# Local softmax: row sums from one VectorE reduction per tile in place of the exponentials' accumulators

## The chip, the cores and the metric

The kernel runs on one NeuronCore of a Trainium2 chip. TensorE (PE) multiplies matrices into PSUM, VectorE (DVE), ScalarE (ACT) and GpSimd (POOL) compute elementwise, and SyncE (SP) issues the transfers. Each engine works through its own instructions in order and waits for the others on semaphores. The metric is the device time of one execution in microseconds (us).

## The reference

The input is 8 sequences of 512 rows with 128 features. Four blocks follow each other, each with a residual and a layer norm in front of it: a small attention of which only the diagonal counts, two layers of a local-attention transformer (8 heads of 64), an attention with 16 heads of 8, and a mixture of 8 experts with a shared one. The change lies in the local attention:

```
bq = q.reshape(b, h, w, WINDOW, d) * QK_SCALE          # WINDOW = 64
bk, bv = (look_around(bk), look_around(bv))            # a window and the one before it: 128 keys
sim = einsum('bhwid,bhwjd->bhwij', bq, bk)
sim = where(mask, -max, sim)
attn = softmax(sim, axis=-1)                           # rows of 128
out = einsum('bhwij,bhwjd->bhwid', attn, bv)
```

The other softmaxes of the program (the diagonal one, the causal one with 16 heads, the router) are computed elsewhere and are not touched.

## The kernel before

The first two blocks are the "front" half (labels F), the last two the "back" half (labels B). Each engine's program is made of two lanes, one a front, one a back half, that work on different sequences at the same time. Each half is cut into named pieces, and a string of the letters F and B for each engine (ORDER) says from which lane the next piece comes. That order is fixed when the program is written; an engine that waits in a piece of one lane does nothing for the other. The strings have three parts: a first stretch, a turn that repeats five times (front of one sequence, back of the one before it), and a last stretch. In the first stretch two fronts run beside each other; in the last, two backs for a part of it.

The local attention of a sequence and layer has 4 tiles m of 128 rows. In one tile 8 heads lie side by side, so its scores are 128 x 1024, in two PSUM banks; four banks hold two tiles. There are 8 x 2 softmaxes, 64 tiles and 512 exponentials of 128 x 128. The pieces of a tile are these:

- sm (PE, lines 536 to 554): mask and scores into the banks of parity m. For m >= 2 it waits until the exponentials of tile m - 2 have left the banks.
- sm (DVE, lines 1108 to 1116): the negated row maxima of the 8 heads (L1111) and their product with the query's inverse norms, the bias of the exponentials (L1115).
- exm0, exm1 (ACT, L870): four exponentials each. Scale and bias are columns of tiles, and accum_out writes each one's row sums into `psum_`. In the trace each is an ACTIVATE and an ACTIVATION_READ_ACCUMULATOR. The eighth raises `l_exp`.
- rp (DVE, L1106): waits for `l_exp`, takes the reciprocals of the 8 sums, 128 x 8, and raises `l_rec`.
- sm, pt1 (POOL, L1400): waits for `l_rec` and multiplies the tile's probabilities by them (128 x 1024), and raises `l_pn`.
- pt (PE, L460): turns the tile's 8 blocks into two banks; pt0 also waits for the exponentials of tile 2, pt1 for those of tile 3, since they use their banks. ACT (L877) and DVE (L1123) copy the two banks out. pt2 and pt3 wait for the copies of the tile before.
- pv (PE) and its copy (ACT, L881), then wo (the output projection, residual added by DVE in L1137 and L1138), mean, var and the feed-forward.

Around them lie, in a turn: while layer 0's softmax runs (.0), the back lane starts a sequence: ln, xn (DVE, L1022; its rstd comes from POOL, L1346), tp and qkv (PE, with copies on ACT, L930 to L935), and parts, parts1 to parts3 (DVE, L1188 to L1197), which split q and k in three bf16 parts and release the transfer of SP (L1477) and behind it 24 more (L1485, L1488) that pack them. max0 to max21 for two rounds (PE scores, DVE row maxima, L1222) use the packed data. While layer 1's softmax runs (.1), the back lane is in its exponentials (ACT, L945, 40 of 128 x 512) and products, then oc (ACT, L948), turn0 to turn3 (PE L736, DVE L1231 and L1233), otp, wo. The rest of a turn is the experts' matmuls (moe, dn) beside the front's feed-forward and the next sequence's embedding and projections.

The program with the lines of the profile:

Of the kernel before, what the change touches and what calls it, by code (L numbers as in the profile page):

```python
# [52 lines left out]
FRONT_ENTERED = 6  # L53
# [3 lines left out]
        "FFFFBFFFBBBBFBFFBFFFFFBBFBFFBFFBFFBBFFFBFFBBBFFFFFFFBBBBBBFFBFFBBFFFFBBFFBFBBFFBFBFFBBFBFFFFBFFFFFBB"  # L57
        "BBBBFBFBBFBBFBFFBFFFFFBBFFBBBFBBBFBBFFFFBFFFFBBFFBFBFBBBFFFBBBBBFBFFFFFFBBBFBBBBFFFFFBFF",
        "FFBBFFFFFFFFFFFFFBBBBFBBBBBBBBBBBBFBBBFBBBFFBFBBFBBBBFBBBBFBFBBBBBFBBBFBBBFBBBBFBBBBBBBBBBBBBFBBBBBF"
        "FBBBFBBBBBBFFBBBFBBFBFBBFBBBBBBBBBBBBBFBBFBBBBBBBFBFBFFFFFFBFBBBFBBBBBBBBFBBFBBBBBFFFBFFFBFBFBBBBFBF"  # L60
        "FBFFFFBBBBBBFBFFBFBFBFBFBBBBBFFFFBFBFFFB",
        "FFBBFFFFBBBBBBBBBBBBBBBBBBBBFBBBBBBBBBBBBBBBBBBFBBBBFBBBBBBBBFBBBFBBBFBBBBBBFBBBFBBBBBFBBBBBBBBBBFBB"
        "BBBBBBBBBBBBBBBBFFBBBBFBBBBFBFFBFBBBBBFFBBBBBBBBBBBFFBBBBBFFBBBBBFBBFBBBBBFFFBBBBBFBBBBFBFFBBBFBFBBF"
        "FFFFFFFFFFBBBBFBBBBBBBBBBBBFBBBBBBBBBBBBBBFBBBBBBFBBBFFBBBFBBBFBBBBFBBBBFBBBBBBBBBFBBBBBBBBFBBBBBBBB"
        "BBBBBBBBBBBBBBBBBBBBBBBBBBBBBBFFFBBFFBBBBFBFBBFFFBBBBBBBBFBFFBBFFBFBFBBFBFFFFBFBBFFBBFFFFBBFFFBBFFBB"
        "FBFFBFFFBFFBFFBBFBBFFFBBFFFFFFFFBFFFFFFFFFFFFFFFFFFFFFFFFFFFFFFFFFFFFFFFFFFFFFFFFFFFFFFFFFFFFFFFFFFF"
# [3 lines left out]
        "FFFFFFBBFFFFFFBBBFFFBFFFBFBBBBFBBFBBFBBBFFFFFFFBFFFFFFFBFBFFBBBBBBBFBFFBBBFBFFBBFBFFFBBFFBFFFFFFFBFB"  # L70
        "FFBBBBFFFFBFBBBFFBBBBFFBBFFFFBFFFBBBBFBFFBBFFFBBBBBFBBBFBBBBFFFFBBBFBFFFFFBFFFFFFBBFBFFFF",
        "FBBFFFFFFFFFFFFFFFFFFFFFFFFFFFFFFBBBBBBBBBBFFBBBBBFBBBBBBFFBBBFBBBBBBFBBFFBBBBBBBFBBBBFFFBFFBFFFFFFF"
        "FBBBBBBFBBFFBFFFBBFBFBFFFFBBFBFFFFFFFFBFFFBFBBFFFF",
        "BBFFFFFFFFFFFFBBFBBBFBBBBBFFBBBBBBBBBBBFBBBBBBBBBBBFBBBBBBBBFBBBFBBFFBBBBBFFFFBBBFFBBFFFFBBFBFFBBFFB"
# [4 lines left out]
        "BFFBFFFFFFFFBFBBBFFBFFFBBFBFFBFFFFBFBBFBBBFBFBFFBBFFFBFFBBFFFFBFBBBBBFBBFBFBBBBFFFBFBFFFFFFFFFBFFBFF"  # L79
        "FFBFFBBBFFBFFBBFBFBBBFFBFBBFFBBBBFBFBBBFBFBFFBFBFFBBFBFBBBBFFFFFFFBFBFFBFFFFFFFFBFBBFBFFFBF",  # L80
        "BFFBBBFBFBFFBFFFFFFFFBBBBBBBBBBBFBBBBBBBBBBFBBFBBFBBBBFBBBBFBFBBBBFFBBBBBBBFFFBFFFFFFFFFFFFFFFFBBBBF"
        "FFBBFFBBBBBBBBBFBFBBBBFFFFBBBFFFBFBBFFBFFFFFFBFBBFFBFBFFFBFFFFBFFBFFBBBFFB",
        "BBBBBBFFFFFFFFBFFBBBBBBBBBBBBBBBBBBBBBBBBBBBBBBBBBBBBBBBBBBBBBFBFFFFBBBBFFFBBBFBBBBBBBFBBFFBBFFBBFBB"
        "BFFBBFBFFBFFBBBBBBFBFBBFFBBFFBBFBFBBBBFFFFFBFFFBBBBFBBBBBBBBBBBBBBBBBBBBBFBBBBBBBBBBBFBBBBBBBBBFFFBF"
        "FFFFFFFBBBBBBFFBBBBBBBFBFFFFFBFBBFBBFFFBFFBFBFBFFBBBFFFFBFFFBFFFFBFFBBFFBFFFFFBFBFFFFFBBBFBFFFFFFFFF"
        "FFFFFFFFFFFFFBFFFFFFFFFFFFFFFFF",
# [1499 lines left out]
```

## Time and profile before

| | before |
|---|---|
| median of 3 runs | 1870.97 us (1866.75 to 1878.17) |
| the profiled execution's own time | 1869.64 us |
| its span (first to last instruction) | 1867.5 us |
| busy: PE, DVE, ACT, POOL | 85%, 62%, 52%, 32% of the span |
| mean granted clock of TensorE | 0.946 |
| chain that ended last: PE, DVE, ACT, POOL | 49%, 19%, 17%, 10% |

The span is what the trace covers; the 2.1 us beside it are launch and end. The chain is followed back from the last instruction, at each step to what released it or to the instruction before it on its engine. Its shares say how long each engine was the one that the end waited for. The five repeated turns show the same pattern; the normalisation that begins one (L1022) starts at 527.96 us and the next at 749.92 us.

### The profile page before, as it was taken

Reading aid. Unit: us, or ns where it says so; the run is one execution under the profiler, and the core shown is the slowest. Engines: PE = TensorE matmul, PEld = TensorE weight load, DVE = VectorE, ACT = ScalarE, POOL = GpSimd, SP = SyncE. Lnnn points to the kernel's source line nnn. Section 1 sums busy time; section 2 is a strip of 40 time slices with the busy share of each in tenths; the row PEclk is TensorE's granted clock in tenths of the full one; section 3 lists DMA queues with packets and bytes.
Section 4 is the critical chain, followed back from the end, with each engine's and each line's share of the span. In section 5 each row is a group of like instructions: output and inputs, shape, how many; then the busy total and the mean of one; then the engine's idle time right before and its main releaser. Section 6 shows DMA issues by size and latency. Waiting matters only on the chain.

```text
span 1867.5 us, 30040 instructions
## 1 busy us (share of the span) xinstructions
...
## 2 busy tenths in 40 slices
...
DMA packets 37293, 80.13 MB, mean 43 GB/s; under 512 B 6782, under 2 KB 22654, under 8 KB 33776
## 3 DMA queue, kind: packets, MB, share of 16 engines
q1 hardware_dynamic: 37152, 78.22, 15.9%
...
## 4 chain that ended last, share of the span: by engine, by line
PE 49%; DVE 19%; ACT 17%; POOL 10%; issue 4%; DMA 0%; SPq 0%; POOLq 0%; DVEq 0%; ACTq 0%
PE ps L455 42%; ACT work L870 6%; PE ps L460 6%; DVE bsmall L1222 5%; POOL fsmall L1346 5%; ACT bigs L945 5%; POOL work L1369 3%; POOL work L1380 2%; DVE fxn L1022 1%; DVE work L1077 1%; DVE fsmall L1111 1%; DVE work L1076 1%; ACT pqs L870 1%; DVE bxn L1022 1%; POOL bsmall L1346 1%
## 5 line engine op out<-in xcount | busy, mean ns | idle before, releaser
L1346 POOL TENSOR_TENSOR fsmall<-fsmall,consts 128x8 f32<-128x8 f32 (+1 forms) x140 | 199.8, 1438 | 328.1 <-DVE fsmall L1016 316.2
L455 PE MATMUL ps<-maskb,identb 128*128 128x128 bf16 (+1 forms) x1118 | 226.4, 239 | 47.4 <-ACT work L870 36.8
L455 PE MATMUL ps<-bxt,mw 128*128 128x512 f32 x504 | 243.5, 600 | 5.9 <-DVE bigs L1318 5.9
L1369 POOL TENSOR_TENSOR work<-work 128x1024 f32<-128x1024 f32 x56 | 132.6, 2368 | 343.9 <-DVE work L1077 343.0
L870 ACT ACTIVATE work<-ps,fsmall 128x128 f32<-128x128 f32 x448 | 200.0, 504 | 32.3 <-DVE fsmall L1115 31.7
L460 PE MATMUL ps<-ident,work 128*128 128x128 f32 x924 | 141.3, 299 | 51.6 <-ACT work L870 31.5
L1222 DVE TENSOR_REDUCE bsmall<-ps 128x1 f32<-128x512 f32 (+3 forms) x308 | 174.8, 633 | 4.8 <-PE ps L455 4.3
L1400 POOL TENSOR_TENSOR work<-work,fsmall 128x1024 f32<-128x1024 f32 x56 | 108.1, 1932 | 214.3 <-DVE fsmall L1106 214.3
L455 PE MATMUL ps<-wqkv,h 128*128 128x512 f32 x336 | 159.4, 604 | 12.5 <-ACT vs L830 6.3
L945 ACT ACTIVATE bigs<-ps 128x512 f32<-128x512 f32 x280 | 145.6, 639 | 25.3 <-PE ps L455 25.0
L460 PEld LDWEIGHTS ps<-ident,work 128*128 128x128 f32 x924 | 114.3, 153 | 83.7 <-ACT work L870 36.3
L455 PEld LDWEIGHTS ps<-maskb,identb 128*128 128x128 bf16 x1152 | 112.0, 100 | 77.2 <-issue 75.8
L967 ACT ACTIVATE bigs<-ps 128x512 f32<-128x512 f32 x126 | 74.7, 597 | 120.4 <-PE ps L455 120.0
L455 PEld LDWEIGHTS ps<-bxt,mw 128*128 128x128 f32 x504 | 88.9, 192 | 91.4 <-issue 76.8
L455 PEld LDWEIGHTS ps<-mw,bigs 128*128 128x128 f32 x1008 | 121.1, 192 | 23.3 <-issue 21.7
L455 PE MATMUL ps<-work,w 128*114 128x512 f32 (+1 forms) x252 | 122.4, 609 | 5.9 <-ACT work L910 3.5
L455 PE MATMUL ps<-pks,pqs 96*128 96x128 bf16 (+3 forms) x448 | 112.1, 314 | 16.8 <-DVE bsmall L1222 10.4
L455 PE MATMUL ps<-mw,bigs 128*128 128x128 f32 x1008 | 123.2, 275 | 0.0
L870 ACT ACTIVATION_READ_ACCUMULATOR work<-ps,fsmall 128x1 f32 x448 | 112.2, 250 | 0.0
L1318 DVE TENSOR_TENSOR bigs<-ps,bigs 128x512 f32<-128x512 f32 x126 | 85.7, 685 | 39.4 <-PE ps L455 24.1
L1111 DVE TENSOR_REDUCE fsmall<-ps 128x8 f32<-128x1024 f32 x56 | 68.3, 1219 | 66.7 <-PE ps L455 66.6
L455 PE MATMUL ps<-pqs,pks 128*128 128x256 bf16 (+3 forms) x420 | 100.4, 299 | 9.6 <-ACT bigs L945 7.8
...
## 6 DMA issues: line engine op xcount, KB each, us to landing
...
```

The source lines that it names most:

```text
L455: return nc.tensor.matmul(o, a, b, start=start, stop=stop, skip_group_check=True)
L460: i = nc.tensor.transpose(bank[:, tt * P:(tt + 1) * P], src(tt), ident[:, :])
L870: i = nc.scalar.activation(R.pr[:, m, a, p, :], R.fb[2 * (m % 2) + a][:, p * P:(p + 1) * P], ACT.Exp, bias=R.pbias[:, m, k:k + 1], scale=R ...
L945: nc.scalar.activation(R.big[n], R.bb[k % 3][:, :], ACT.Exp).then_inc(R.c_e.sem, 1)
L967: nc.scalar.activation(R.silu[e % 2][c], R.bb[n % 3][:, :], ACT.Silu).then_inc(R.m_silu.sem, 1)
L1022: i = ts(xn[:, tt, :], src[:, tt, :], mv[:, tt, 0:1], rs[:, 1, tt:tt + 1], ALU.subtract, ALU.mult)
L1111: nc.vector.tensor_reduce(R.pmax[:, m, :], R.fpair[m % 2].rearrange("p a (c b) -> p (a c) b", b=P), AX.X, ALU.max, negate=True).then_inc(R ...
L1222: nc.vector.tensor_reduce(R.cmax[:, r, heads[0]:heads[-1] + 1, t], R.bb[k % 4][:, 0:cols * len(heads)].rearrange("p (a b) -> p a b", b=col ...
L1318: tt_(R.hid[e % 2][c], R.bb[n % 3][:, :], R.silu[e % 2][c], ALU.mult).then_inc(R.m_hid.sem, 1)
L1346: return nc.gpsimd.tensor_tensor(out, x, consts[:, k:k + 1].broadcast_to([x.shape[0], x.shape[1]]), op)
L1369: nc.gpsimd.tensor_tensor(R.qk[:, m, :], R.qk[:, m, :], R.part[m % 2], ALU.add).then_inc(R.l_add.sem, 1)
L1400: nc.gpsimd.tensor_tensor(p3, p3, R.prec[:, m, :].unsqueeze(2).broadcast_to([P, HEADS, P]), ALU.mult).then_inc(R.l_pn.sem, 1)
```

## The change

In the local softmax the exponentials no longer have accum_out. In rp, before the reciprocals, DVE sums the tile's 8 x 128 probabilities from SBUF with one tensor_reduce, 128x8 from 128x1024, raises a count of its own semaphore chain and waits for it. The chain's count per sequence grows by 4 per layer. Nothing else is computed otherwise.

```diff
-        self.fv, self.fp = sig("front_vector", FRONT_ENTERED + 4 * LAYERS, kind=Chain), sig("front_gpsimd", 2, kind=Chain)
+        self.fv, self.fp = sig("front_vector", FRONT_ENTERED + 8 * LAYERS, kind=Chain), sig("front_gpsimd", 2, kind=Chain)
...
                             i = nc.scalar.activation(R.pr[:, m, a, p, :], R.fb[2 * (m % 2) + a][:, p * P:(p + 1) * P], ACT.Exp,
-                                                     bias=R.pbias[:, m, k:k + 1], scale=R.rn[:, m, 2 * p + a:2 * p + a + 1],
-                                                     accum_out=R.psum_[:, m, k:k + 1])
+                                                     bias=R.pbias[:, m, k:k + 1], scale=R.rn[:, m, 2 * p + a:2 * p + a + 1])
                     i.then_inc(R.l_exp.sem, 1)
...
                 def reciprocals(m):
                     dve.wait_ge(R.l_exp.sem, R.l_exp.at(s, 4 * l + m + 1))
+                    nc.vector.tensor_reduce(R.psum_[:, m, :], R.pr[:, m, :, :, :].rearrange("p a c b -> p (a c) b"), AX.X,
+                                            ALU.add).then_inc(R.fv.sem, R.fv.one())
+                    dve.wait_ge(R.fv.sem, R.fv.now(s))
                     nc.vector.reciprocal(R.prec[:, m, :], R.psum_[:, m, :]).then_inc(R.l_rec.sem, 1)
```

The strings of all five engines are new as well, in all three stretches. Their pieces are the same, and each lane keeps its own order; only the interleaving differs. Read as pieces, the places of a turn that the text speaks of are these (the piece in brackets is the front's or the back's, F or B):

```
ACT before: (F)ex00.0 (B)tp (B)qkv (F)ex01.0 (F)ex10.0 (F)ex11.0 (F)ex20.0 (F)ex21.0 (F)ex30.0 (F)ex31.0 (F)pt0.0 (F)pt1.0
ACT after:  (F)ex00.0 (F)ex01.0 (B)tp (F)ex10.0 (B)qkv (F)ex11.0 (F)ex20.0 (F)ex21.0 (F)ex30.0 (F)ex31.0 (F)pt0.0 (F)pt1.0

DVE before: (B)ln (F)sm0.0 (F)sm1.0 (B)xn (B)parts (B)parts1 (F)rp0.0 (B)parts2 (F)sm2.0 (B)parts3 (F)rp1.0 (F)sm3.0 (B)va (F)rp2.0 (F)pt0.0 (F)rp3.0 (F)pt1.0
DVE after:  (B)ln (F)sm0.0 (B)xn (F)sm1.0 (F)rp0.0 (B)parts (B)parts1 (B)parts2 (B)parts3 (F)sm2.0 (F)rp1.0 (F)sm3.0 (F)rp2.0 (F)pt0.0 (B)va (F)rp3.0 (F)pt1.0

PE, DVE before: (F)wo1.0 (F)mean.0 (B)max0.0 (B)max1.0 (B)max2.0 (B)max3.0 (then PE: (F)var.0)
PE, DVE after:  (F)wo1.0 (B)max0.0 (B)max1.0 (F)mean.0 (B)max2.0 (B)max3.0 (PE's (F)var.0 two pieces later)

DVE before: (F)sm3.1 (F)rp2.1 (B)turn0 (B)turn1 (B)turn2 (B)turn3 (F)pt0.1 (F)rp3.1 (F)pt1.1 (B)wo (F: pt2.1 after it)
DVE after:  (F)sm3.1 (F)rp2.1 (B)turn0 (B)turn1 (F)pt0.1 (B)turn2 (B)turn3 (F)rp3.1 (F)pt1.1 (B)wo (F)pt2.1
PE before:  (B)turn2 (B)turn3 (F)pt0.1 (B)otp (F)pt1.1 (B)wo (F)pv0.1 (F)pt2.1
PE after:   (B)turn2 (F)pt0.1 (B)turn3 (F)pt1.1 (B)otp (F)pv0.1 (B)wo (F)pt2.1

PE before:  (B)dn2 (F)w2.1 (B)moe40g (F)out
PE after:   (F)w2.1 (B)dn2 (F)out (B)moe40g
SP before:  (B)dn1 after (B)dn0, then (F)ln; (F)v23.0 before (B)dn7
SP after:   (F)ln after (B)dn0, then (B)dn1; (F)v23.0 after (B)dn7
```

## Rows read from the trace of the kernel before

**Rows 1.** The page, part 4: the whole chain by engine and line, shares of the span.

```profile
PE 49%; DVE 19%; ACT 17%; POOL 10%; issue 4%; DMA 0%; SPq 0%; POOLq 0%; DVEq 0%; ACTq 0%
PE ps L455 42%; ACT work L870 6%; PE ps L460 6%; DVE bsmall L1222 5%; POOL fsmall L1346 5%; ACT bigs L945 5%; POOL work L1369 3%; POOL work L1380 2%; DVE fxn L1022 1%; DVE work L1077 1%; DVE fsmall L1111 1%; DVE work L1076 1%; ACT pqs L870 1%; DVE bxn L1022 1%; POOL bsmall L1346 1%
```

**Rows 2.** Busy time by window: window, its us, engines busy (instructions), clock, DMA.

```profile
547.00:553.00 6.00, 5.10 (x46) 4.65 (x47) 1.03 (x3) 2.50 (x7) 1.90 (x1) 0.50 0.73 124
527.96:749.92 221.96, 194.33 (x1446) 114.93 (x1454) 138.93 (x319) 122.59 (x285) 73.02 (x48) 0.96 0.17 42
624.00:650.00 26.00, 21.30 (x271) 13.40 (x268) 10.02 (x23) 22.80 (x81) 8.11 (x5) 0.93 0.01 2
565.00:600.00 35.00, 32.15 (x164) 15.34 (x161) 34.55 (x63) 13.52 (x19) 3.99 (x2) 1.00 0.05 11
```

**Rows 3.** Chain of waits, 527 to 566 us (layer 0): shares, then start, us, what.

```profile
by line: PE ps L455 39.6%; ACT work L870 22.9%; PE ps L460 14.6%; DVE fsmall L1111 3.2%; DVE bxn L1022 2.9%; POOL bsmall L1346 2.6%; issue 2.5%; DVE h L1138 1.8%; DVE work L1142 1.8%; DVE h L1137 1.8%; DVE bsmall L1222 1.5%; ACT bxt L930 1.
...
527.96 1.12 DVE bxn L1022 x4
...
535.13 5.30 ACT work L870 x24
...
544.22 3.64 ACT work L870 x16
...
547.90 1.97 PE ps L460 x8
...
551.78 1.77 PE ps L460 x8
...
554.63 1.02 PE ps L460 x8
...
563.56 1.14 PE ps L455 x2
...
564.73 0.69 DVE work L1142
```

**Rows 4.** Timeline of ACT: start, us, line, operation, tiles, shapes; three neighbours.

```profile
540.80 0.45 ACT L870 ACTIVATE work<-ps,fsmall 128x128 f32<-128x128 f32 x1
541.14 0.20 ACT L870 ACTIVATION_READ_ACCUMULATOR work<-ps,fsmall 128x1 f32 x1
541.23 0.45 ACT L870 ACTIVATE work<-ps,fsmall 128x128 f32<-128x128 f32 x1
```

**Rows 5.** Line L1084, a sum on DVE from SBUF: ns min/median/max, first and last start.

```profile
L1084 DVE TENSOR_REDUCE fsmall<-work x56: 1205/1210/1221, 38.9 to 1563.7; 128x16 f32<-128x1024 f32 x56
```

**Rows 6.** Timelines of ACT, DVE and POOL in layer 0's softmax; idle time before in brackets.

```profile
530.09 0.59 ACT L930 COPY bxt<-ps 128x512 f32<-128x512 f32 x1 [2.10 <-PE ps L460]
...
534.54 0.59 ACT L935 COPY ctmps<-ps 128x512 f32<-128x512 f32 x1 [1.11 <-PE ps L455]
...
547.88 0.20 DVE L1106 RECIPROCAL fsmall<-fsmall 128x8 f32<-128x8 f32 x1 [2.43 <-ACT work L870]
...
548.16 1.90 POOL L1400 TENSOR_TENSOR work<-work,fsmall 128x1024 f32<-128x1024 f32 x1 [1.30 <-DVE fsmall L1106]
```

**Rows 7.** Chain of waits in the last stretch: parts to parts3 without a gap.

```profile
1420.76 0.70 DVE bigs L1188
...
1424.70 1.14 DVE fsmall L1111
```

**Rows 8.** Chain of waits, 618 to 660 us (layer 1): shares, then pieces.

```profile
by line: PE ps L455 42.1%; ACT work L870 16.7%; PE ps L460 12.7%; ACT bigs L945 11.6%; issue 3.3%; DVE fsmall L1111 2.9%; DVE bxn L1233 2.9%; DVE bsmall L1231 2.6%; ACT ctmps L948 2.5%; PE ps L736 1.6%; ACT qts L881 1.4%; DVE fsmall L1115 0
...
625.95 3.27 ACT work L870 x15
...
638.99 4.29 PE ps L455 x57
...
647.23 1.53 PE ps L460 x12
...
650.80 1.02 PE ps L460 x8
```

More of the change, by code:

```diff
@@ L56 @@
     "tensor": (
[L57 to L66, printed above, removed]
+        "FFFFFFFBBBBBFBFFFFBFFFBFBBFBFBFBFBFFFFFFFBBFBFFFBBFBFFBBBBFFBFBFBFFFBBFFFBFBBFFBFFBFFBBBFFFFBFFFFFBB"
+        "BBBBFBFBFBBFBFBFFFBFFFFFBBFBBBBBFBBBFFFFFFBFBFBFFBFBBFFFFBBBBBBBFBFFFFFFBBBBFBBFFBBFFFFF",
+        "FFBBFFFFFFFFFFFFBBFBBBBFBBBBBBBBBBBBFBFBBBFBBFBFFBBBBFBBBBFBBBFBBFBFBBBBBBFBBBBFBBBBBBBBBBBBBBBBBFFB"
+        "BBBFFBBBBBBBFBBFFBBBFFBBFBBBBBBBBBFBBBBBBBFBBBBBFBFBFBFFFFFBFBBBBFBBBFBBBBBBFBBBBBFFFFFFBFBFBBBBBFBF"
+        "FBFFFFBBBBBBFBFFBFBFBFBBFBFBBFBFFBBFFFFB",
+        "FBBFFFFFFBBBBBBBBBBBBBBBBBBBBBBBBBBBFBBBBBBBBBBBBBBFBBBBBBBBBBBFBFBBBFBBBBBBBFBBBFBBBBFBBBBBBBFBBBBB"
+        "BBBBBBBBBBBBBBBBFFBBBBFBBBBFBFBFFBBBBBFFBBBBBBBBBBBBBFFBBBBBFFBBBBBFBBBBBBBFFFBBFFBFFFBBBBBBBBFBFBBF"
+        "FFFFFFFFFFBBBBFBBBBBBBBBBBFBBBBBBBBBBBFFBBBBBBBBBBBBBFBBBBFFBBFBBFBBBBBBFBBBBBBBBBBBBBBFBBBFBBBBBBBB"
+        "BBBBBBBBBBBBBBBBBBBBBBBBBBBBBBFFFFBFBBFFFBBBFBBFFBBBBBBFFBBBBBBFBFFFFBBFFBBFBBFBBFBFFBFFBBBFBFFFBFFF"
+        "BFFBBFBFFFFBFFFFBBBBFFBFFFFFFFFFBFFFFFFFFFFFFFFFFFFFFFFFFFFFFFFFFFFFFFFFFFFFFFFFFFFFFFFFFFFFFFFFFFFF"
         "FFFFFFFFFFFFFFFFFFFFFFFFFFFFFFFF",
@@ L69 @@
     "scalar": (
[L70 to L74, printed above, removed]
+        "FFFFFFBBFFBBFFFFFBFBFFFBFBBBFBFFBBBBBBFFFFBFFFBFFFFBBFFFBFFFFBBBBBBFBFFBBBFBFFBBBBFFFFFFFFBBFFFFFBFB"
+        "FFBBBBFFFFFBBBBFFFBFBBBBFFFFFBFFBBBFBBBFBFBFFFBBBBBFBBBFFBBFFBFBBBBFBFFFFBFFFFFFFBBFBFFFF",
+        "FFBFBFFFFFFFFFFFFFFFFFFFFFFFFFFFBFBBBBBBBBBFFBBBBBBBFBBBBFFBBBBBBFFBBBBBFFBBBBFBBBBBBBFFFBFFFBFFFFFF"
+        "FBBBBBBFBBFFBFFFBBFBFBFFFFBBBFFFFFFBFFFFFFBFBFFBFF",
+        "BBFFFFFFFFFFFFFBBBBBBBFFBBBBFBBBBBBBBBBFBBBBBBBBBBBFBBBBBBBBFBBBBFFBFBBBBFBBFBFBFFFBFFBFBFFBBFBFBFBF"
         "BBFBBFFFFBBFFFFFFFFFFFFFFFFFFBBBBBBBBBBBBBBBBBBFBBBFBBBBBBBBBBBBBBBBBBBBBBBBBBBBBBBBBBBBBBBBBBBBFFFF"
```

24 lines of the change are left out of this document (12 added, 12 removed).

## The prediction

> **What bounds the kernel now.** I read the chain of waits by line first. PE holds 49% of it and ACT 17%, and the local exponentials (L870, tiles work and pqs together) 7% of the span, or about 131 us of 1867.5 [rows 1]. So they do set the end for a part of the time. Next comes one turn by windows: in 222 us PE is busy for 194, DVE for 139, ACT for 123 [rows 2]. PE leaves 28 us idle per turn, and a faster ACT can only win there.
>
> The chain by windows shows where. Around layer 0's softmax L870 holds 22.9% of 39 us, 8.9 us; around layer 1's 16.7% of 42 us, 7.0 us [rows 3, 8]. That is 15.9 us per turn, 80 us in five turns, and leaves 51 us for the first and last stretch. In layer 1 ACT is busy for 22.8 of 26 us while DVE has 16 us free [rows 2]: there work goes from a full engine to an idle one. In the stretch behind layer 0's softmax it is the other way round, DVE is busy for 34.55 of 35 us [rows 2], but none of the new reductions lies there.
>
> **What one exponential gives back.** An exponential starts, its accumulator read 0.34 us later, the next exponential 0.09 us after that: a pitch of 0.43 [rows 4]. The read lasts 0.20 us but overlaps on both sides. Without it the next exponential should start where the read started, so the gain is 0.09 us of 0.43 (21%), not the 0.20 of its row. 512 of them are 46 us of ACT in all, 0.72 us per tile.
>
> The pitch without accumulator isn't in the trace, so bounds: a read that hides wholly in the next one's start-up gives 0; its whole duration gives 0.20. I take 0.09, the distance between the starts. The Trainium skill (ScalarE: Activation LUTs, section What ACT_TABLE_LOAD costs) gives an ACTIVATE 186 ns and 0.833 ns a column, 93 ns more for each operand that is a pointer, and 93 ns of overlap. For 128 columns with two pointers its estimate is a pitch of 386 ns, so 0.05 us gained instead of 0.09, and with it the ACT part of the sums below would be a little over half.
>
> **What the reduction costs.** A sum of 128x1024 from SBUF is in the trace: 1.21 us, also when repeated [rows 5]. With a semaphore wait of 0.07 it adds about 1.3 us between a tile's last exponential and its reciprocals: 64 x 1.3 = 83 us of DVE against 46 us saved on ACT. The change loses engine time, and what counts is where each lies. Bounds on the path: 0 where a wait hides it, 1.3 each where not.
>
> **Layer 0 in a turn, step by step** (old times). The back's xn ends at 529.08 [rows 3]; moved ahead of sm1, it keeps that time, since it waited for POOL anyway. Tile 1's maxima come after it, 1.2 us, and its bias at about 530.5. ACT has holes: tp's copy at 530.09 after 2.10 idle, the last of qkv's at 534.54 to 535.13 [rows 6]. The new order puts ex01 before tp and ex10 before qkv. Four exponentials at 0.34 are 1.37 us, so ex01 ends near 528.9 and ex10 near 532.0, both in holes. rp0's reduction (530.6 to 531.9) is hidden by DVE's wait for qkv.
>
> From 535.13 the steps are: parts to parts3, 3.94 us without a gap [rows 7], to 539.1, so SP's transfer leaves some 2.3 us earlier than before (parts3 came after sm2 there). ex11 ends at 536.4. Maxima and bias of tile 2, 1.45 us, to 540.55; its exponentials, 8 x 0.34, to 543.3; meanwhile rp1 (1.3 + 0.2) to 542.0 and tile 3's maxima to 543.5. Exponentials of tile 3 to 546.3. DVE behind it: rp2 to 545.1, pt0's copy 0.69, va 0.68, rp3 to 547.9. PE's pt1, which starts at 547.90 now [rows 3], waits only for tile 3's exponentials and starts at 546.4: **1.5 us** earlier. rp3's result now leaves DVE at 547.9, where the reciprocal alone is now at 547.88 [rows 6]; POOL's 1.90 us bring it to 549.9, and pt3 needs it at 554.63 at present [rows 3], 553.1 in the new order. So 3 us cover it. Without that cover it would cost 1.3 us a softmax.
>
> **mean.0 behind max1.0.** Now DVE is idle for the 1.14 us of PE's mean product and then does L1142 [rows 3] before the run of maxima that fills it [rows 2]. In the new order the first two maxima fill that hole: **1.2 us** off a stretch where DVE is the bound, provided that the packed data have landed; their transfer leaves 2.3 us earlier than now. Ends: 0 and 1.2; I take 1.2, since DVE is at 99% there.
>
> **Layer 1.** From 625.95 to 638.5 ACT doesn't pause; the chain runs through 16 exponentials, 10 of the back and a copy [rows 8]. 16 x 0.09 = 1.5 us less, so PE's sm3.1 (638.99) comes 1.5 us earlier, and behind it the products, oc and the turns. otp now waits at 647.23 for the four DVE pairs of turn; there pt0's copy (0.69) is new in front of turn2. pt1.1 goes ahead of otp, which fills PE's wait. rp3 runs after turn3, about 646.4 to 647.9, then pt1's copy to 648.6; pt2.1 can start there, where it is at 650.80 now [rows 8]: 2.2 us. I take **2.0**; bounds 0.7 (the exponentials' 1.5 less the copy) and 2.2. rp2 lies ahead of turn0, covered by oc on ACT, which itself waits for PE.
>
> **The other moves.** w2.1 ahead of dn2 and out ahead of moe40g start the next embedding up to 2 us earlier; the transfers of v23.0 leave after dn7 and are needed 25 us later. I cost them at nothing, hidden by the experts' matmuls, with bounds of -1 and +1 us a turn; the same for every other move of a piece by one or two places.
>
> **The sum.** A turn: 1.5 + 1.2 + 2.0 = 4.7 us; five of them 23.5. First and last stretch: 51 us of exponentials in the chain x 0.21 = 10.7, less one reduction of 1.4 on the path in each of their six softmaxes (8.4), since two fronts share DVE at the start and nothing fills a wait near the end: 2.3. Together 26 us off the profiled execution's 1869.64, which is 1.3 below the median: **1844 us**, 1.4% faster.
>
> **The rivals.**
> *Absorbed.* What is gained at the softmaxes ends in a wait for something else: packed data of the second round, POOL's norms that the next back sequence waits for, or PE's fixed order. For it: PE is busy for 88% of a turn [rows 2]; 4.7 of 28 idle us is a lot to ask. Then the two layers keep a third, 8 us, and it gives about 1862. Chance 0.27.
>
> *The reduction ahead of the copies (slower).* Place: rp2 and rp3, in front of pt0's and pt1's copy and of turn0. If PE is waiting there already, each softmax pays for two reductions, 2.6 us x 16 = 42, against 28 us from the exponentials (21% of 131): +14, and 1884. With the third reduction (turn0 behind rp2 in layer 1, copies in layer 0) it is 35, and 1905. It decides when a tile's exponentials end less than 1.5 us ahead of the copy of the tile before. Against it speaks POOL's slack of 4.6 us between 550.06 and 554.63 [rows 3, 6]. The Trainium skill (VectorE: DVE Perf Modes, Rules for kernel authors) warns of just this: it calls `tensor_reduce` on the hot path the slowest operation of the engine and advises restructuring. The trace agrees on its price, 1.21 us for 1024 columns, but not on its being hot here. Chance 0.16.
>
> *The clock.* From 547 to 553 the granted clock is 0.50, the lower of its two levels, 1.2 GHz, after a softmax in which PE mostly idled [rows 2]. Turning eight tiles takes 1.97 and 1.77 us there and 1.02 at the upper level [rows 3]; with the products between them I estimate 2.5 us lost per turn. If the shorter idle time lets the clock stay up, five turns give 12 us more: 1832. If a fall comes where there is none now, as much is lost: 1856. Chance 0.07 for the gain; PE waits nearly as long as before, so I expect the same level.
>
> *No effect from the read.* If exponentials keep their pitch, the moves alone are left: about 1 us of layer 0's 1.5, and 1.2: 1858. Within the chances of the first rival.
>
> **How the numbers follow.** Forecast 0.50, absorbed 0.27, slower 0.16, clock 0.07. What can be told from no change is 1%, 18.7 us: faster is below 1852, slower above 1890. The forecast's own range is 1828 to 1856 (the bounds above: five times -3 to +2, and the ends' 10); a fifth or less of it is over 1852. Faster 0.45 + 0.07 + a part of absorbed = 0.55; slower 0.13, since two thirds of that rival's span from 1884 to 1905 lie beyond 1890 (0.11), and moves that I priced at nothing can go that way (0.02); same 0.32. The range takes the absorbed case and most of the slower one: 1820 to 1884.
>
> **What would show it.** Right: starts of L870 0.34 us apart; ACT busy some 45 us less, DVE some 75 more; 64 new reductions of about 1.21; per turn 217 us between two L1022 of the back; L870 under 5% of the chain. A chain that goes through the new reduction, or through L1106 and L1400, makes the second rival right; idle time of DVE in front of L1222, or new time of POOL in the chain, the first. The forecast fails if the turn's 222 us stand although ACT gets its 0.09 back.

## The result, and the profile after

The kernel after takes 1867.38 us (median of 11 runs, 1862.92 to 1870.98), the kernel before 1874.27 on the same chip (11 runs, 1866.75 to 1879.73). The ratio is 0.9963, 95% interval 0.9950 to 0.9977: 0.4% faster, where 1.4% was forecast. The profiled execution took 1865.29 us, its span is 1863.5 (before: 1869.64 and 1867.5). The forecast's terms add up to 26 us; 4.0 us of span came in the two traces, and 6.9 us between the two medians. The accounts below are of traces, one for each kernel, and a trace can lie some us beside its kernel's median: m2's (below) is the fastest of its 12 runs, 9.6 us under its median.

The page of the kernel after: busy time by engine, then the chain that ended last by engine and by line. L1348 was L1346 before, L1224 was L1222, L944 was L945, L1113 was L1111; L1105 is the new reduction.

```profile
PE 1598.5 (86%) x11565; PEld 934.8 (50%) x11632; DVE 1239.7 (67%) x2636; ACT 926.7 (50%) x1751; POOL 594.0 (32%) x401
...
PE 47%; DVE 23%; ACT 14%; POOL 12%; issue 4%; DMA 0%; SPq 0%; POOLq 0%; DVEq 0%; ACTq 0%
PE ps L455 42%; POOL fsmall L1348 5%; DVE bsmall L1224 5%; ACT bigs L944 5%; PE ps L460 4%; POOL work L1371 3%; ACT work L870 3%; DVE fsmall L1113 2%; POOL work L1382 2%; POOL bsmall L1348 1%; DVE fsmall L1105 1%; DVE bxn L1021 1%; DVE work L1076 1%; DVE work L1075 1%; DVE fxn L1021 1%
```

Against [rows 1] the exponentials of tile work fell to 3% of the chain. ACT has 42 us less to do (968.6 before), DVE 89 more (1150.5 before), of which the 64 reductions are 78. DVE took over the share of the chain that ACT gave up.

The timeline of ACT in the kernel after, beside [rows 4]: start, length, line, operation, tiles, shapes, count.

```profile
978.13 1.16 ACT L870 ACTIVATE work<-ps,fsmall 128x128 f32<-128x128 f32 x3
```

Three exponentials take 1.16 us, and one lasts 0.474 (median). So two pitches are 0.69 and one is 0.34, as forecast. The new reduction: durations min/median/max, first and last start.

```profile
L1105 DVE TENSOR_REDUCE fsmall<-work x56: 1204/1212/1222, 85.4 to 1602.0; 128x8 f32<-128x1024 f32 x56
L1105 DVE TENSOR_REDUCE bsmall<-pqs x8: 1206/1220/1220, 115.0 to 248.3; 128x8 f32<-128x1024 f32 x8
```

64 of them at 1.21 us, the duration of [rows 5]. Both prices were right. (The rows of tile pqs are those of the other front in the first stretch, which keeps its probabilities there.) Next the chain of layer 0's softmax, the part of the after kernel that answers to [rows 3]: start, length, what.

```profile
544.25 0.70 DVE bigs L1190
...
546.97 1.23 DVE bigs L1199
548.19 1.14 DVE fsmall L1113
...
549.60 1.14 DVE fsmall L1105
...
550.96 1.10 DVE fsmall L1113
...
553.00 2.91 ACT work L870 x8
...
555.95 1.97 PE ps L460 x8
...
571.20 0.03 DVE bsmall L1224
...
572.52 0.69 DVE work L1144
```

Before, 20 exponentials stood in this chain ([rows 3] counts 24 and 16 instructions, half of them accumulator reads); now there are 8. In their place DVE works from parts (L1190) to tile 3's bias without a gap, one new reduction among its work. From parts to the turning of pt1 (L460) it is 11.70 us; before it was 12.7 (the back's parts at 535.2, the turning at 547.90 [rows 3]). The turning still takes 1.97 us. The clock there begins at its lower level as before; over 6 us from the turning's start its mean is 0.62 (0.55 before), and the next turning takes 1.38 us (1.77 before). And the max in front of L1144 is the move of mean.0: it now starts before the mean's subtraction.

One row of that chain was in no sum. Tile 3's bias, a product of 128x8 numbers on DVE (L1117), takes 0.17 us elsewhere and 0.18 at this place before the change. Here it takes 0.80, and tile 3's exponentials wait for it. The timeline shows POOL's multiplication of tile 1 beside it:

```profile
551.04 1.90 POOL L1402 TENSOR_TENSOR work<-work,fsmall 128x1024 f32<-128x1024 f32 x1 [8.33 <-DVE fsmall L1108]
...
552.15 0.80 DVE L1117 TENSOR_TENSOR fsmall<-fsmall 128x8 f32<-128x8 f32 x1
```

The product ends 0.02 us behind POOL's instruction. It is so in each of the five turns, 0.63 us each. In this trace 11 of the 64 products are that long (0.49 to 1.57 us); each ends 0.02 to 0.03 us behind a POOL instruction of 128x512 or 128x1024, while the 53 short ones at most begin in the last 0.05 us of one. No run here moves POOL's instruction away, so that it holds DVE up is read from these rows, not tried.

In layer 1 (beside [rows 8]) the chain holds four exponentials where it had 16, and one reduction:

```profile
638.09 1.40 ACT work L870 x4
...
647.87 1.14 DVE fsmall L1105
```

**Where the time went.** I cut both traces at landmarks: the second x2 of the front (the end of the part in which two fronts run side by side), the parts of each back sequence, and within a turn the attention's residual, layer 1's first sm and the first reduction of the back's route. Means over the five turns, in us:

| stretch | before | after | difference | forecast |
|---|---|---|---|---|
| turn: parts to wo1.0 (layer 0's softmax) | 26.5 | 25.8 | -0.8 | -1.5 |
| turn: wo1.0 to sm0.1 (maxima, mean.0) | 62.6 | 62.0 | -0.6 | -1.2 |
| turn: sm0.1 to route (layer 1's softmax) | 34.4 | 32.0 | -2.4 | -2.0 |
| turn: route to the next parts | 97.7 | 97.4 | -0.3 | 0 |
| one turn | 221.3 | 217.1 | -4.1 | -4.7 |
| five turns | 1106.3 | 1085.7 | -20.6 | -23.5 |
| start to second x2 | 294.1 | 301.3 | +7.2 | +0.7 |
| second x2 to the first turn's parts | 20.4 | 24.6 | +4.2 | 0 |
| last stretch | 446.8 | 451.9 | +5.1 | -3.0 |
| span | 1867.5 | 1863.5 | -4.0 | -25.8 |

(The rows are rounded one by one, so they add up to the span within 0.1.)

The forecast gave its ends together, -2.3. I split that here: in the chain before, L870 holds 7.9% of the first 294.1 us, 23.2 us, of which 21% are 4.9; four softmaxes there at 1.4 are 5.6; the rest of the 51 us and the other two softmaxes are the last stretch. The turns gave nearly what was forecast. The ends took 16.6 us back (20.6 less 4.0).

### The profile page after: what moved, and what is told of

Read it like the earlier page. It is cut to its first block, busy times and chain, and to the rows that moved or that the text cites. A ratio compares the mean times of both kernels' runs of the same rounds, so it can differ in the third digit from the quotient of the medians.

```text
span 1863.5 us, 29596 instructions
## 1 busy us (share of the span) xinstructions
PE 1598.5 (86%) x11565; PEld 934.8 (50%) x11632; DVE 1239.7 (67%) x2636; ACT 926.7 (50%) x1751; POOL 594.0 (32%) x401
## 4 chain that ended last, share of the span: by engine, by line
PE 47%; DVE 23%; ACT 14%; POOL 12%; issue 4%; DMA 0%; SPq 0%; POOLq 0%; DVEq 0%; ACTq 0%
PE ps L455 42%; POOL fsmall L1348 5%; DVE bsmall L1224 5%; ACT bigs L944 5%; PE ps L460 4%; POOL work L1371 3%; ACT work L870 3%; DVE fsmall L1113 2%; POOL work L1382 2%; POOL bsmall L1348 1%; DVE fsmall L1105 1%; DVE bxn L1021 1%; DVE work L1076 1%; DVE work L1075 1%; DVE fxn L1021 1%
## 5 line engine op out<-in xcount | busy, mean ns | idle before, releaser
L1348 POOL TENSOR_TENSOR fsmall<-fsmall,consts 128x8 f32<-128x8 f32 (+1 forms) x140 | 200.1, 1440 | 330.5 <-DVE fsmall L1015 310.9
L870 ACT ACTIVATE work<-ps,fsmall 128x128 f32<-128x128 f32 x448 | 164.0, 493 | 71.1 <-DVE fsmall L1117 70.4
L460 PE MATMUL ps<-ident,work 128*128 128x128 f32 x924 | 140.6, 298 | 50.2 <-ACT work L870 42.4
L1224 DVE TENSOR_REDUCE bsmall<-ps 128x1 f32<-128x512 f32 (+3 forms) x308 | 175.3, 631 | 7.5 <-PE ps L455 6.8
L455 PE MATMUL ps<-wqkv,h 128*128 128x512 f32 x336 | 163.4, 618 | 14.1 <-ACT vs L830 8.8
L1402 POOL TENSOR_TENSOR work<-work,fsmall 128x1024 f32<-128x1024 f32 x56 | 106.2, 1897 | 216.1 <-DVE fsmall L1108 216.1
L944 ACT ACTIVATE bigs<-ps 128x512 f32<-128x512 f32 x280 | 146.1, 635 | 24.1 <-PE ps L455 23.7
L966 ACT ACTIVATE bigs<-ps 128x512 f32<-128x512 f32 x126 | 75.3, 598 | 156.6 <-PE ps L455 155.9
L460 PEld LDWEIGHTS ps<-ident,work 128*128 128x128 f32 x924 | 114.1, 153 | 76.7 <-ACT work L870 51.2
L455 PEld LDWEIGHTS ps<-maskb,identb 128*128 128x128 bf16 x1152 | 113.4, 101 | 63.4 <-issue 61.9
L455 PE MATMUL ps<-work,w 128*114 128x512 f32 (+1 forms) x252 | 128.7, 636 | 10.1 <-ACT work L909 7.0
L455 PEld LDWEIGHTS ps<-wqkv,h 128*128 128x128 f32 x336 | 61.3, 195 | 91.0 <-issue 58.7
L1075 DVE TENSOR_TENSOR work<-ps,sinT 128x512 f32<-128x512 f32 x112 | 76.5, 683 | 38.3 <-PE ps L455 34.5
```

Source lines behind the costliest of these rows:

```text
L455: return nc.tensor.matmul(o, a, b, start=start, stop=stop, skip_group_check=True)
L460: i = nc.tensor.transpose(bank[:, tt * P:(tt + 1) * P], src(tt), ident[:, :])
L870: i = nc.scalar.activation(R.pr[:, m, a, p, :], R.fb[2 * (m % 2) + a][:, p * P:(p + 1) * P], ACT.Exp, bias=R.pbias[:, m, k:k + 1], scale=R ...
L944: nc.scalar.activation(R.big[n], R.bb[k % 3][:, :], ACT.Exp).then_inc(R.c_e.sem, 1)
L966: nc.scalar.activation(R.silu[e % 2][c], R.bb[n % 3][:, :], ACT.Silu).then_inc(R.m_silu.sem, 1)
L1075: tt_(p4, q4[:, :, ::-1, :], t4.unsqueeze(1).broadcast_to([P, HEADS, 2, 32]), ALU.mult)
```

## The experiments

Twelve kernels. The first four part the change: m1 has the new arithmetic in the old order, m2 the old arithmetic in the new order. The edits are shown shortened: {before} and {after} stand for the order strings of the two kernels, and ... for text left out.

**m1_math_old_order** is the kernel after with the order strings of the kernel before.

```diff
-ORDER = {after}
+ORDER = {before}
```

> Reductions in place of accumulators, all strings as before the change. Theory (edges): the turns owe their 4.1 us each to both, exponentials 0.09 us shorter and pieces moved; the reduction alone in the old places sits in front of parts2 and of the copies and takes a good part back, so a turn loses nothing or gains up to 2 us (219.5 to 222 between two starts of parts), and the first stretch, where two fronts share DVE, gets longer by some 5 us: 1870 to 1880 us, ratio 0.998 to 1.004 to the kernel before. Rival (order): if the new places cost the first and last stretch their time and the reduction costs nothing, this kernel keeps the turns' gain of the exponentials (3 us each) with no loss at the edges: 1850 to 1858.

**m2_new_order_acc** is the kernel before with the order strings of the kernel after.

```diff
-ORDER = {before}
+ORDER = {after}
```

> Accumulators kept, strings of the changed kernel. Theory (edges): of a turn's 4.1 us about 2.5 come from places (exponentials in ACT's holes, mean.0 behind max1.0), so turns of 219 us; turn 1 loses 4 us to the clearing of the packed keys in front of sm1.0; the first stretch loses less than with reductions, 2 us against 7: 1866 to 1872 us. Rival (order is the loss at the edges): first stretch again 7 us longer than before, last one 5, so 1872 to 1880.

Measured: m1 1881.48 us, ratio 1.0056 (1.0038 to 1.0073); m2 1880.6 us, 1.0038 (1.0021 to 1.0054). Each half alone is slower than the kernel before, the whole is faster. m1 was expected at 1870 to 1880 and its turns at 219.5 to 222, about what came. m2 was expected at 1866 to 1872 and lies just above the range of its rival (the order alone costs the ends their time, 1872 to 1880). m2's trace is of a run of 1870.96 us, so where the other 9.6 us of its median arise no trace shows; its runs above 1880 us have granted clocks of 0.938 to 0.942, the traced one 0.943. Before, m1, m2 and the kernel after have turns of 221.3, 221.8, 219.8 and 217.1 us: +0.5 and -1.5 alone, -4.1 together. The second x2 stands at 294.1, 300.6, 299.2 and 301.3: there each half costs about what both cost. By the stretches of the table above m1 has 26.8, 64.0, 32.2 and 98.8 us: it gains 2.2 in layer 1's softmax and loses 0.3, 1.4 and 1.1 in the others. Against the same order without any sums (o1, below: 24.9, 63.3, 32.1, 98.4) the reductions cost most in layer 0's softmax, 1.9 us. m1's chain there:

```profile
986.23 0.70 DVE bigs L1190
...
986.96 1.23 DVE ctmps L1193
988.18 1.14 DVE fsmall L1105
...
990.11 1.14 DVE fsmall L1113
...
991.88 1.14 DVE bigs L1199
993.02 1.14 DVE fsmall L1105
...
994.39 1.10 DVE fsmall L1113
...
996.42 2.91 ACT work L870 x8
...
999.37 1.97 PE ps L460 x8
```

rp0.0 stands behind parts1 there, so two reductions lie between parts and pt1: 13.1 us against 11.7. And in each of m1's turns POOL's multiplication lies beside the bias products of two tiles, which take 0.54 and 0.81 us.

**m3_clear_after_maxima** changes the kernel after in one place. In the first turn only, DVE does sm1.0 before the back's xn, as in the kernel before. The first xn also clears the packed keys' tiles (clear_packed_k, four fills of constants), which the forecast had overlooked.

```diff
-    for lane in first + turn * TURNS + last:
+    for lane in first + ("BFFBF" + turn[5:] if turn.startswith("BFBFF") else turn) + turn * (TURNS - 1) + last:
```

> The changed kernel with one place changed back in the first of the five turns, on DVE alone: sm1.0 ahead of xn, whose piece there also clears the packed keys (four fills of 1.76 us). Theory: the clearing in front of sm1.0 holds the exponentials of tile 1; parts of the first back sequence comes 4 us earlier and nothing behind gives it back: 1863 us, 4 less than the changed kernel. Rival: the time before that turn's packed data bound it anyway, and it stays at 1867.

**m4_hybrid** goes on from there: the first and last strings are those of before, and in those stretches the exponentials keep their accumulators, with a fill of one column in place of the reduction. The turns are those of m3.

```diff
+keeps_sums = lambda R, s: R.count == 1 or s in (0, TURNS + 1)
-                                                     bias=..., scale=...)
+                                                     bias=..., scale=..., **({'accum_out': R.psum_[:, m, k:k + 1]} if keeps_sums(R, s) else {}))
-                    nc.vector.tensor_reduce(R.psum_[:, m, :], ...)
+                    (nc.vector.memset(pause[:, :], 0.0) if keeps_sums(R, s) else nc.vector.tensor_reduce(R.psum_[:, m, :], ...))
```

> First and last stretch with the strings of before and with accumulators (sequence 0, and those whose softmaxes run outside the five turns); the five turns with the strings and reductions of the changed kernel, the clearing placed as in m3. Theory: the turns keep their gain (5 x 4.1) and the losses at the edges, 7.4 + 4 + 5, go: 1848 to 1853 us, 1.1 to 1.3% faster than before. Rival: the edges' losses come from the turns' pieces next to them and are not cured by it: 1860 to 1864.

m3: 1856.66 us, ratio 0.9920 (0.9904 to 0.9936), where 1863 was expected. m4: 1857.89, 0.9928 (0.9914 to 0.9942). The chain of the kernel after at the place that m3 changes:

```profile
313.56 1.76 DVE pks L987
...
315.70 1.78 DVE pks L987
...
317.95 1.76 DVE pks L991
...
320.09 1.76 DVE pks L991
...
321.89 1.24 DVE fsmall L1113
...
323.42 1.51 ACT work L870 x4
```

Four fills, 8.3 us with their waits, stand between the back's xn and sm1.0 (L1113), and tile 1's exponentials start only at 323.42. In m3 the first parts come at 322.9 instead of 325.9: 3.0 us. But m3's span is 9.4 us shorter (1854.1). The other 6.1 came in the last stretch, 445.8 us instead of 451.9, though its strings and instructions are the same. m4 was expected at 1848 to 1853: its second x2 did go back to 295.4, but its last stretch took 449.9 with before's strings and accumulators, where before takes 446.8.

**The clock in the last stretch.** The last stretch of m3, of the kernel after and of n4 (below, the same strings there): from:to and length, then busy time and count of PE, PEld, DVE, ACT and POOL, the mean granted clock, the DMA engines' share and GB/s.

```profile
1408.30:1854.10 445.80, 378.18 (x2621) 223.07 (x2637) 256.34 (x594) 174.24 (x325) 52.47 (x38) 0.93 0.19 48
```

```profile
1411.60:1863.50 451.90, 385.64 (x2621) 227.57 (x2637) 256.02 (x594) 174.69 (x325) 52.78 (x38) 0.91 0.19 47
```

```profile
1407.70:1859.40 451.70, 388.06 (x2639) 227.72 (x2637) 256.52 (x594) 174.63 (x325) 52.47 (x38) 0.91 0.19 47
```

The instructions are the same (a few records of PE are missing from the first two traces), DVE and ACT are busy for the same time, and PE takes 7 to 10 us more at the lower mean clock. PE's idle time does not grow with it: 67.6 us in m3, 66.3 in the kernel after. Nor do the traces differ from the start of the stretch. For its first 209 us m3, after, n4 and n6 have the same busy times within 0.2 us and a mean clock of 0.90 each (n4 has ten records of PE more, 1.5 us). The rest, in m3 and in the kernel after:

```profile
1617.30:1854.10 236.80, 202.28 (x1278) 117.19 (x1284) 132.82 (x332) 84.13 (x147) 8.53 (x10) 0.96 0.16 42
```

```profile
1620.60:1863.50 242.90, 209.81 (x1278) 121.87 (x1284) 132.48 (x332) 84.50 (x147) 8.81 (x10) 0.92 0.16 42
```

All of the difference lies there: 6.1 us of length, 7.5 of PE's busy time. I summed the time that each trace spends at the lower level (clock 0.50) in this stretch. Over all traces, in order: n7 51.4 us low and 443.8 long; m2 54.6, 445.0; m3 58.0, 445.8; before 61.5, 446.8; n5 61.9, 450.4; n1 64.9, 448.8; n3 64.9, 448.3; m4 65.1, 449.9; n2 68.7, 454.2; m1 72.2, 450.8; o1 75.3, 450.0; after 78.5, 451.9; n4 78.5, 451.7; n6 78.5, 452.2. The length follows the clock, about 0.3 us for each us at the lower level, and hardly the order, the accumulators or the reductions. At 64.9 us low, n1 without any sums and n3 with them differ by 0.5 us. n2 (reductions doubled) and n5 (whose parts comes late) stand out, by about 5 and 3, m4 and o1 by +1.7 and -1.1. So in the last stretch the change itself is worth nothing within about 1 us, and the +5.1 goes with the clock: 17 us more at the lower level are 5.1 at 0.3. The same shows between runs: the 17 runs of the kernel before beside m1 to m4 reach from 1867.68 us (clock 0.945) to 1878.48 (0.940), with a correlation of -0.81 between time and clock; in its runs beside the other experiments it is -0.84, -0.60 and -0.59. But the clock isn't a matter of the single run alone. All 6 runs of m3 (1852.75 to 1860.64 us, mean clock 0.944) lie below all 11 of the kernel after (1862.92 to 1870.98, mean clock 0.940), so m3's better clock comes again in its other runs, which have no trace.

**n1_no_sums and n2_double_sums** take m3 and leave the sums out, or make each twice.

```diff
-                    nc.vector.tensor_reduce(R.psum_[:, m, :], R.pr..., AX.X, ALU.add).then_inc(R.fv.sem, R.fv.one())
+                    nc.vector.memset(R.psum_[:, m, :], 4.0).then_inc(R.fv.sem, R.fv.one())
```

> This is the kernel after with the first turn's clearing of the packed keys behind sm1.0 (m3_clear_after_maxima, 1856.7 us), and its row sums are left out: a small fill of psum_ stands where the reduction over 128x1024 was, with the same signal and wait. Theory (one reduction of 1.2 us per layer lies on the path in a turn, three to six in the first stretch, where two fronts share VectorE): the turns go from 217.2 to about 214.8 us, the first x2 from 301.5 to about 295, the kernel to about 1838. Rival (in the turns the new order hides the reductions behind other work; only the first stretch pays): turns 217.2, first x2 about 295, kernel about 1850. Rival (reductions hidden everywhere, the lost time is only the order's): 1855 to 1858.

```diff
+                    for _ in range(2):
                         nc.vector.tensor_reduce(R.psum_[:, m, :], R.pr..., AX.X, ALU.add).then_inc(R.fv.sem, R.fv.one())
                         dve.wait_ge(R.fv.sem, R.fv.now(s))
```

> The same base (1856.7 us), with each reduction over 128x1024 made twice, one after the other, each with its signal and wait: 1.3 us more at each tile. Theory (one reduction per layer on the path in a turn): turns 217.2 to about 219.8 us, first x2 301.5 to about 308, the last stretch some 3 more, kernel about 1879. Rival (hidden in the turns): turns 217.2, kernel about 1866. Hidden everywhere: 1855 to 1858.

What n1 computes is not the softmax: a constant takes the place of the sums, and only its time is of use. n1: 1843.24 us, ratio 0.9850 (0.9821 to 0.9879), between the theory's 1838 and the rival's 1850. n2: 1907.53, 1.0208 (1.0186 to 1.0229). Turns of 216.0, 217.1 and 222.3 us with none, one and two; the second x2 at 295.8, 301.5 and 311.4. The first reduction costs 1.1 us a turn, the second 5.2: eight reductions a turn, most of them hidden, but with little slack left behind them. n2's chain in layer 0, where three tiles' pairs have come onto it:

```profile
1008.13 1.14 DVE fsmall L1106
1009.30 1.23 DVE fsmall L1106
...
1012.75 1.14 DVE fsmall L1106
1013.91 1.23 DVE fsmall L1106
...
1016.52 1.14 DVE fsmall L1106
1017.68 1.23 DVE fsmall L1106
...
1019.75 1.34 PE ps L460 x8
```

Neither theory had this bend. For one reduction the truth lies between 0 and one a layer; for two the expectation (219.8) was 2.5 short. n2's kernel time, 1907.53, is far above the expected 1879.

**n3, n5 and n7** undo one move of the new order each, in m3's turns.

**n3_mean_first**, on PE and DVE (PE's var.0 ahead of max4.0, DVE's ahead of max11.0 as well):

```diff
-(F)wo1.0 (B)max0.0 (B)max1.0 (F)mean.0 (B)max2.0
+(F)wo1.0 (F)mean.0 (B)max0.0 (B)max1.0 (B)max2.0
```

> The same base (1856.7 us), with one move of the new order undone in the turns: TensorE's and VectorE's steps mean.0 and var.0 stand ahead of the attention maxima again (mean.0 before max0.0, var.0 before max4.0 on TensorE and before max11.0 on VectorE), as in the kernel before. Theory of the prediction (mean.0 behind max1.0 takes 1.2 us of waiting off the path in each turn): turns 217.2 to 218.4 us, kernel about 1863. Rival (the wait is covered elsewhere, the move is worth nothing): 1856 to 1858.

**n5_copies_first**, on ACT:

```diff
-(F)ex00.0 (F)ex01.0 (B)tp (F)ex10.0 (B)qkv (F)ex11.0
+(F)ex00.0 (B)tp (B)qkv (F)ex01.0 (F)ex10.0 (F)ex11.0
```

> The base (the kernel after with the first turn's clearing behind sm1.0, 1856.7 us), with one move of the new order undone in the turns: ScalarE's exponential steps ex01.0 and ex10.0 stand behind the back's two copies tp and qkv again, as in the kernel before. Theory of the prediction (in layer 0 the shorter exponentials give 1.5 us per turn because they are laid ahead of the copies): turns 217.2 to about 218.7 us, kernel about 1864. Rival (it does not matter on which side of the copies they stand): 1856 to 1858.

**n7_vector_layer0_old**, on DVE:

```diff
-(B)xn (F)sm1.0 (F)rp0.0 (B)parts (B)parts1 (B)parts2 (B)parts3 (F)sm2.0 (F)rp1.0 (F)sm3.0 (F)rp2.0 (F)pt0.0 (B)va (F)rp3.0
+(F)sm1.0 (B)xn (B)parts (B)parts1 (F)rp0.0 (B)parts2 (F)sm2.0 (B)parts3 (F)rp1.0 (F)sm3.0 (B)va (F)rp2.0 (F)pt0.0 (F)rp3.0
```

> The same base (1856.7 us), with VectorE's steps of the front's layer 0 at the start of a turn in the order of the kernel before (xn behind sm1.0, rp0.0 behind parts1, sm2.0 ahead of parts3, rp1.0 behind it, va ahead of rp2.0), the reductions kept. Theory of the prediction (in layer 0 the new order is what keeps the reduction's 1.2 us off the back's copies): turns 217.2 to 218.4 to 219 us, kernel 1862 to 1866. Rival (these moves are worth nothing, as they were priced): 1855 to 1858.

n3: 1866.61 us, 0.9970 (0.9957 to 0.9983), turns 219.0: +1.9 for a move that was priced at 1.2 (expected 218.4). n7: 1861.86, 0.9932 (0.9912 to 0.9952), turns 218.4: +1.3, as expected. n5: 1881.25, 1.0034 (1.0012 to 1.0055), turns 220.8 (expected 218.7): +3.7, of which 2.5 lie between route and the next parts. n5's chain tells why, and it isn't only ACT:

```profile
983.73 0.59 ACT ctmps L934
984.31 1.42 ACT work L870 x4
...
985.75 1.23 DVE fsmall L1105
...
987.21 0.57 DVE bigs L1190
```

ex01.0 stands behind qkv's copy (L934), rp0.0 waits for ex01.0, and parts (L1190) stands behind rp0.0 on DVE. So parts waits 2.9 us after its data are there. The move on ACT and the move of rp0.0 ahead of parts need one another, so the three prices (6.9 together) may not be added: with reductions the whole order is worth 4.7 (221.8 to 217.1).

**n4_best** and **n6_first_without** put before's first strings in front of the rest of m3, with accumulators there. n4 kept them in only one of the two fronts of the first stretch; n6 has them in both.

```diff
+keeps_sums = lambda R, s: R.count == 1                 (n4)
+keeps_sums = lambda R, s: R.count == 1 or s == 0       (n6)
```

> The first stretch's strings of the kernel before with its accumulators there (no reductions in the first stretch), the turns' and the last stretch's strings and the reductions of the kernel after, and the first turn's clearing behind sm1.0. Theory (the first stretch's loss comes from the reductions and the order there, the rest is as in m3): first x2 about 295 where m3 had 301.5, kernel 1850 to 1855. Rival (what the first stretch gives is lost again in the last part, where the clock falls for 10 or for 24 us): 1856 to 1860.

> n4_best kept its accumulators in one only of the two fronts that share the first stretch; here both have them, so that no reduction stands in the first stretch, whose order is the kernel before's. Turns and last stretch are those of the kernel after, reductions there, the first turn's clearing behind sm1.0. Theory (each front's reductions cost the first stretch about 3 to 5 us): first x2 295.4 us as in m4_hybrid, parts of the first turn at 317.2, turns 217.2, the last stretch 446 to 452 by the clock: kernel 1850 to 1856. Rival (what the first stretch gives back is lost again in the turns): 1858 or more.

n4: 1861.92 us, 0.9952 (0.9936 to 0.9968). n6: 1859.31, 0.9919 (0.9901 to 0.9936). Their second x2 stands at 300.6 and 297.9. m4 and n6 run the same instructions up to there, and m4 was at 295.4. Their first 233 us:

```profile
0.00:233.00 233.00, 175.89 (x1357) 100.05 (x1366) 152.09 (x307) 140.63 (x378) 137.61 (x95) 0.95 0.17 47
```

```profile
0.00:235.20 235.20, 181.16 (x1357) 103.03 (x1366) 152.86 (x307) 140.81 (x378) 137.73 (x95) 0.92 0.17 47
```

Same counts; PE 5.3 us busier at clock 0.92 in n6 than at 0.95 in m4, and 2.2 us later at the first x2. Up to the second x2 n6 has 47.8 us at the lower level and m4 34.1, and is 2.5 us later. So a difference of that size between two traces of the first stretch need not come from an edit. n6 is not told apart from m3; it came out in its rival's range (1858 or more). n4 is slower than m3 by about 0.3% and missed both its ranges, 1850 to 1855 and 1856 to 1860.

**o1_old_order_no_sums** is m1 with its sums left out, to see what the shorter exponentials alone give. Its edit is n1's.

> The order strings of the kernel before, exponentials without accumulators, and the row sums left out: a small fill of psum_ stands where the reduction was (m1_math_old_order without its reductions). It tells what the shorter exponentials alone give, stretch by stretch. Theory formed from the runs so far (in the first stretch TensorE and the other front fill what the exponentials leave, so the shorter ones are worth next to nothing there, and m1's 300.6 us are the price of its reductions): first x2 at 294 to 295 us as in the kernel before, the last stretch 445 to 451 by the clock, the turns at about 217 to 219. Rival (the forecast's step: 21% of the exponentials in the chain come off in the first stretch too): first x2 at 289 us or earlier.

1855.17 us, 0.9884 (0.9861 to 0.9907). With it there is a table of two orders by three ways to sum, here the second x2 and the mean turn, in us:

| | accumulators | no sums | reductions |
|---|---|---|---|
| second x2, old order | 294.1 (before) | 290.0 (o1) | 300.6 (m1) |
| second x2, new order | 299.2 (m2) | 295.8 (n1) | 301.5 (m3) |
| turn, old order | 221.3 | 218.6 | 221.8 |
| turn, new order | 219.8 | 216.0 | 217.1 |

My theory for o1 (the shorter exponentials give nothing in the first stretch) fell. They give 4.1 us; the forecast's step gives 4.9 there (its rival in the expectation, 289 or earlier, was missed by 1). Taken as they stand, the 16 reductions of the first stretch cost 10.6 us in the old order, not 5.6, and 5.7 in the new order, which costs 5.8 of its own. The clock has a part in these differences. Up to the second x2 before spends 41.0 us at the lower level, o1 30.7, m1 41.0, m2 and n1 44.4, m3 and after 47.8. Between o1 and n1 lie 13.7 us, as many as between m4 and n6, which ran the same instructions and are 2.5 us apart. With that as the price of the clock (an estimate from one pair, 0.18 us for each us at the lower level) the exponentials give some 2 us, the reductions cost some 9 and 5, and the new order some 3. Before and m1 have the same 41.0 and are 6.5 us apart, so that much of the start's loss is not the clock.

m1's chain from 175 to 256 us shows the reductions of both fronts, six in 72 us:

```profile
179.86 1.23 DVE fsmall L1105
...
191.74 1.14 DVE fsmall L1105
...
226.91 1.14 DVE bsmall L1105
...
234.04 1.23 DVE bsmall L1105
...
238.79 1.14 DVE bsmall L1105
...
251.43 1.14 DVE bsmall L1105
```

## Why the prediction was right, and where it was wrong

The forecast was 1844 us and 1.4%; 1867.38 and 0.4% came. Both prices and the repeated turns came out nearly as said; the step for the first and the last stretch, and what the moved xn does in the first turn, did not.

**Right: both prices.** The pitch fell from 0.43 to 0.34 us. The reduction lasts 1.21, and from its start to the reciprocals it is 1.25 (1.3 said). The Trainium skill's estimate for the pitch (ScalarE: Activation LUTs, What ACT_TABLE_LOAD costs), 386 ns, was not met: two exponentials follow one another in 343.

**Right: the turns.** 4.1 of 4.7 us each. The lines that the forecast named are there: 217 us a turn, L870 at 3% of the chain, 64 reductions. The cover of rp3 held: L1402 (L1400 before) is not in layer 0's chain behind the softmax. Layer 0 gave 0.8 of 1.5 and the mean's stretch 0.6 of 1.2, though undoing that move costs 1.9. Layer 0's sum counts 11.3 us from parts to the turning of pt1, and 11.7 came; the 0.63 us by which tile 3's bias is longer are in none of its terms. Layer 1 gave 2.4 of 2.0. Nearly all of that comes from the shorter exponentials, since the old order reaches 32.2 us there too (m1).

**Not so: the rivals.** "Absorbed" gives 1862, nearer to 1867 than the forecast, and would look right by the time alone. But the turn's 222 us didn't stand, and what the turns gave was not lost in them. The reductions ahead of the copies decide in the old order: there they cost 3.2 us a turn (218.6 to 221.8; the rival's price is 5.2), and m1 is slower than before. In the new order they cost 1.1. The forecast's sign for this rival was a chain that goes through the new reduction, and it does (L1105, 1% of the span, one in each chain above); n1 shows that this is worth 1.1 us a turn, not 5.2. The clock is still at its lower level when pt1's turning starts, as forecast; where it matters is the last stretch.

**Wrong, first: "First and last stretch ... less one reduction of 1.4 on the path in each of their six softmaxes ... 2.3".** This step failed by 6.5 us at the start. It forecast +0.7 up to the second x2, and +7.2 came. The exponentials' gain was about as said (4.1 of 4.9, some 2 with the clock taken out). What was missing is that the forecast read the strings of a turn and took the first stretch's new strings at nothing: n1 against o1, both without sums, puts them at +5.8, of which some 2.5 may be the clock. And it counted one reduction a softmax where two fronts share DVE; in the old order that is 10.6 us (some 9 without the clock) instead of 5.6. The two don't add: in the new order the reductions cost 5.7, about as forecast. Which pieces of the first strings cost the time was not tried.

**Wrong, second: "moved ahead of sm1, it keeps that time".** That holds in four turns. In the first turn the same piece clears the packed keys, 8.3 us on DVE, and the move puts them in front of sm1.0. The stretch up to parts became 4.2 us longer, and m3 takes 3.0 of the 4.2 back. This can be read in the code that is called from xn; the forecast looked at a later turn only.

**Wrong, third: the last stretch.** Forecast -3.0; measured about 0 for the change, and +5.1 with the clock. That the lower clock makes it is shown by three traces with the same instructions there. What makes the clock stay at the lower level 20 us longer in one than in another isn't shown: the stretch starts within 4 us of the same time in all three, and they run alike for its first 209 us.

Of the 21.8 us between forecast and trace, 2.9 are the turns, 6.5 the first stretch, 4.2 the clearing and 8.2 the last stretch. The range that the forecast gave its main case, 1828 to 1856, is also narrower than its own bounds: five times -3 to +2 and the ends' 10 add up to 25 us on one side and 20 on the other, where the range has 16 and 12.
